# A bidirectional Mamba block with quantized feed-forward: transposes first in TensorE's positions, four evictions behind the next exponential

## What is computed

```python
xz = x @ win.T
u, z = jnp.split(xz, 2, axis=-1)
...
u = jax.nn.silu(jnp.transpose(uc, (0, 2, 1)) + bconv)
dbc = u @ wx.T
...
delta = jax.nn.softplus(dt @ wdt.T + bdt)
A = -jnp.exp(Alog)
dA = jnp.exp(delta[..., None] * A)
dBu = (delta * u)[..., None] * Bm[:, :, None, :]

def step(h, t):
    dA_t, dBu_t, C_t = t
    h = dA_t * h + dBu_t
    return (h, jnp.einsum('bdn,bn->bd', h, C_t))
...
y = jnp.swapaxes(ys, 0, 1) + u * Dp
y = y * jax.nn.silu(z)
return y @ wout.T
```

## Time and profile before

| | us |
|---|---|
| median of 3 runs | 7538.34 |
| lowest, highest | 7523.53, 7542.44 |
| profiled execution | 7536.37 |
| span of the profiled execution | 7534.1 |

### The profile page before, as it was taken

The page is one execution under the profiler, slowest core; times in us unless marked ns, Lnnn a source line. Parts: engine busy times, 40 slices in busy tenths (PEclk is TensorE's granted clock), DMA queues, the critical chain, the costliest instruction groups (busy, mean ns, idle before and its releaser), DMA issues. The chain is left out here.

```text
span 7534.1 us, 111379 instructions
## 1 busy us (share of the span) xinstructions
PE 6807.4 (90%) x32682; PEld 4050.3 (54%) x32682; DVE 6775.4 (90%) x9064; ACT 6168.4 (82%) x13081; POOL 6966.7 (92%) x3774
## 2 busy tenths in 40 slices
PE   6899999999999999999999889999998999998889
PEld 3455555555555555555555555555555555555455
DVE  2799999999999999999999999999999999999766
ACT  1788888888888888888888888888888888888645
POOL 0899999999999999999999999999999999999678
PEclk8999999999999999999999999999999999999999
DMA  8444455444444554444444544444445444444555
GB/s 258 142 138 134 129 147 150 111 139 135 137 134 130 145 151 111 138 138 136 135 131 141 151 116 132 139 137 133 131 141 151 118 131 140 138 133 129 157 187 173
DMA packets 605402, 1064.06 MB, mean 141 GB/s; under 512 B 113584, under 2 KB 221872, under 8 KB 596336
## 3 DMA queue, kind: packets, MB, share of 16 engines
q1 hardware_dynamic: 602704, 1055.81, 48.1%
q10 hardware_dynamic: 2080, 1.05, 0.0%
HBM read 926.59 MB, written 130.03 MB: 140 GB/s over the span
## 5 line engine op out<-in xcount | busy, mean ns | idle before, releaser
L692 POOL TENSOR_TENSOR dBu<-Bb,du 128x1024 f32<-128x1024 f32 x2048 | 4796.6, 2365 | 4.8 <-DMA Bb<-bc_scratch 4.4
L807 ACT ACTIVATE scans<-delta,A 128x512 f32<-128x512 f32 x4096 | 2748.1, 698 | 204.6 <-DVE hC L1162 199.7
L1146 DVE TENSOR_TENSOR_SCAN scans<-scans,state,dBu 128x512 f32<-128x512 f32 x2016 | 2535.4, 1278 | 327.5 <-ACT scans L807 325.0
L1146 DVE TENSOR_TENSOR_SCAN dBu<-scans,state,dBu 128x512 f32<-128x512 f32 x1568 | 1957.0, 1260 | 10.2 <-ACT scans L807 10.2
L1019 PE MATMUL yT<-ident,hC 128*128 128x128 f32 x9216 | 1398.9, 283 | 268.2 <-DVE hC L1162 266.1
L1162 DVE TENSOR_TENSOR hC<-scans,Cb 128x512 f32<-128x512 f32 x2304 | 1553.4, 678 | 4.7 <-PE yT L1019 4.7
L702 POOL TENSOR_TENSOR hR<-dBu,Cb 128x512 f32<-128x512 f32 x1024 | 1307.0, 1276 | 196.0 <-DVE dBu L1146 194.9
L1019 PEld LDWEIGHTS yT<-ident,hC 128*128 128x128 f32 x9216 | 1086.7, 145 | 551.2 <-DVE hC L1162 337.4
L774 ACT ACTIVATE turned<-bg,CT 128x128 f32<-128x128 f32 x3072 | 878.5, 372 | 225.9 <-PE bg L996 225.4
L1012 PE MATMUL bg<-u,comb 128*128 128x512 f32 x2112 | 992.4, 596 | 54.4 <-ACT pre L783 51.6
L973 PE MATMUL bg<-hT,win_z 128*128 128x512 f32 x2048 | 971.7, 597 | 0.0
(11 more groups left out here) (161 smaller groups left out, 7892.4 us busy)
## 6 DMA issues: line engine op xcount, KB each, us to landing
comb<-pre_scratch SPq DMA_DIRECT2D x1040, 256.0 KB, 4.6
Bb<-bc_scratch SPq DMA_DIRECT2D x264, 512.0 KB, 7.1
Cb<-bc_scratch SPq DMA_DIRECT2D x264, 512.0 KB, 7.2
win_u<-in_win SPq DMA_DIRECT2D x264, 256.0 KB, 4.6
pre_scratch<-pre SPq DMA_DIRECT2D x264, 256.0 KB, 3.7
comb<-comb_scratch SPq DMA_DIRECT2D x66, 1024.0 KB, 8.4
win_z<-in_win SPq DMA_DIRECT2D x257, 256.0 KB, 2.7
part_scratch<-pre SPq DMA_DIRECT2D x132, 256.0 KB, 2.0
```

The lines of the kernel that those rows point to most:

```text
L692: pool.tensor_tensor(dBu[:, ring(g, q)], Bb[:, 2 * q:2 * q + 2, :], du[:, j % 2, :].unsqueeze(1).broadcast_to([P, 2, T]), ALU.mult).then_i ...
L807: act.activation(place(n)[:], delta[:, j % 2, :], ACT.Exp, scale=A[:, i % 2, j * N + n:j * N + n + 1]).then_inc(dA_made, 1)
L1146: nc.vector.tensor_tensor_scan(to, place(n)[:], dBu[:, ring(g, q), k, :], state[:, c:c + 1] if i % CH_SEQ else 0.0, ALU.mult, ALU.add).the ...
```

## The change

Two things change, in order alone.

First, `IN_ORDER` puts the entries Y and T of the schedule ahead of all others, and both `background` and the numbering (`BY_END`) go by it. Y was first in its positions already. A T moves ahead of what shared its position in 15 of 24 cases: T1, T17, T33, T49, T65, T81 and T97, which are the first of their tiles and come right after a Y in bank 2, and T5, T9, T25, T37, T57, T101, T105 and T117. T9 is now also taken by ScalarE ahead of O0. Which bank and which earlier user a piece waits for stays as it was (`LAST` still goes by `SCHEDULE`).

Second, `LATER` names the evictions that fall on a table visit, except in the last position: O2 (position 15), U1 (23), C6 (47) and T101 (53). They are now made in the next position, between its two exponentials.

```diff
--- before.py
+++ after.py
@@ -83,7 +83,8 @@
 AT = {name: at for name, at, bank in SCHEDULE}
 BANK = {name: bank for name, at, bank in SCHEDULE}
 
-BY_END = [name for name, at, bank in sorted(SCHEDULE, key=lambda entry: entry[1][-1])]
+IN_ORDER = sorted(SCHEDULE, key=lambda entry: entry[0][0] not in "YT")
+BY_END = [name for name, at, bank in sorted(IN_ORDER, key=lambda entry: entry[1][-1])]
 NUM = {name: e for e, name in enumerate(BY_END)}
 
 LAST = {}
@@ -104,6 +105,7 @@
 GATED = {7: (("Z", 0),), 15: (("Z", 1),), 23: (("Z", 2),), 31: (("C", 0), ("Z", 3)), 39: (("C", 2), ("Z", 4)),
          47: (("C", 4), ("Z", 5)), 53: (("C", 6), ("Z", 6)), 63: (("Z", 7),)}
 assert all(TAKE[f"{kind}{m + (kind == 'C')}"] < p + (kind == "Z") and (kind == "C" or p // NQ == m) for p in GATED for kind, m in GATED[p])
+LATER = [name for name in BY_ACT if TAKE[name] in GATED and TAKE[name] < POS - 1 and name not in URGENT]
 assert sorted(m for p in GATED for kind, m in GATED[p] if kind == "C") == list(range(0, MT, 2))
 assert sorted(m for p in GATED for kind, m in GATED[p] if kind == "Z") == list(range(MT))
 
@@ -891,6 +893,9 @@
                         keep_state(g, j, 2 * q - KEPT_BEHIND)
                         if q == 1:
                             take_yT(g - 1, ready(i - 1, "Y6") if j == 0 else ready(i, f"Y{(j - 2) % MT}"))
+                        for name in LATER:
+                            if p == TAKE[name] + 1:
+                                take(name, i, s, g)
                         if p == TAKE[f"D{m}"] + 1:
                             step_exp(freed(i, f"D{m}"))
                         if p == TAKE[f"D{m}"] + 2:
@@ -911,7 +916,7 @@
                         if p == 12:
                             act.wait_ge(cur_loaded, i * 16 + 32)
                         for name in BY_ACT:
-                            if p == TAKE[name] and name not in URGENT:
+                            if p == TAKE[name] and name not in URGENT and name not in LATER:
                                 take(name, i, s, g)
                         for tt in range(TT):
                             if p == NORM_POS + tt:
@@ -1037,7 +1042,7 @@
 
             def background(i, s, p):
 
-                for name, at, own in SCHEDULE:
+                for name, at, own in IN_ORDER:
                     bank, kind, k = bg[own], name[0], int(name[1:] or 0)
                     for piece in range(len(at)):
                         if at[piece] != p:
```

## The result

The changed kernel takes 7623.3 us (median of 4 runs, 7618.6 to 7631.5), against 7530.9 for the kernel before in the same comparison (7523.1 to 7542.4): the ratio is 1.0124 [1.0107, 1.0141], 92 us slower. The forecast was 7583, so sign and order are right, and the loss is twice the 45 us of the sum. The profiled execution took 7618.6 (span 7616.4).

What follows compares the result with a forecast made beforehand. The period was taken to be set by TensorE's queue, ScalarE's behind it, then VectorE's scans. Earlier transposes, lost cover and moved evictions summed to +1.4 us per chunk, 45 us over 32 chunks: 7583, with 8 in 10 from 7469 to 7680.

Steps and rivals of the forecast that it cites:

- the walk: Tile-by-tile sum through chunk 10 of VectorE's shift against before, positive later, ending at +1.4 us per chunk.
- The term of tile 4: Tile 4: Z4's 1.72 us comes behind T65's gate wait and ahead of U4, taking position 40 from -0.8 to +0.85.
- a rival of its own: TensorE's clock drops after new waits in tiles 1, 4 and 5: 106 us on top, 7689; chance 0.10.
- below 0.96 in the chunks: Sign that the prediction is wrong: the granted clock falls below 0.96 in the chunks.
- The term of tile 0: Tile 0: first transpose finds its gate open, T9 overtakes the last four matmuls of O0; VectorE's shift -0.6 us.
- some 4 to 5: Sign: TensorE's transposes wait some 4 to 5 us per chunk for VectorE's gate, 1.3 or more in tile 1.
- (a): Transposes come 1.72 us earlier; ScalarE's waits of 2.75 and 1.86 us at positions 14 and 30 shrink to under 1.
- (c): Four evictions step behind an exponential; VectorE's waits at positions 16, 24, 48, 54 shrink, O3's wait on TensorE does not.
- costed at 0.1: Tile 6: T105, ahead of a piece of X, waits for T101 to be taken; X is needed only next tile.
- The bound: Upper limit for gate waits at tile heads: 4.7 us per chunk (150 us) if no later slack takes any.
- The faster rival: Idling in tiles 4 and 5 does not reach the scans: -2.15 us per chunk, 7469; chance 0.22.
- the one without change: Only one idling, tile 4's or 5's, reaches the scans; without tile 5's 1.2, +0.2 us per chunk, 7545; chance 0.16.

Runs made afterwards that it cites:

- n = 1 alone: Kernel before, with only the first transpose of each tile moved ahead and the evictions left as they were: 7830.0 us, ratio 1.0403.
- n = 5 and 9 alone: Kernel before, with only the transposes that are not first in their tile moved ahead and the evictions left as they were: 7431.7 us, ratio 0.9866.
- The covered run: Kernel before with only T65 ahead of Z4, plus two matmuls of Z4 made once more ahead of T65: 7573.6 us, ratio 1.0054.
- the best kernel: Kernel before with T5, T9, T25, T37, T57, T101, T117 ahead and U1, C6, T101 evictions moved; T105 behind X: 7388.9 us, ratio 0.9814.

## Why the prediction was right, and where its size was off

VectorE's shift at the places of the walk, forecast and measured (mean over chunks 2 to 29):

| place | forecast | measured | change since the place above: forecast, measured |
|---|---|---|---|
| tile 0, position 8 | -0.6 | +0.14 | -0.6, +0.1 |
| tile 1, position 16 | -0.15 | +0.52 | +0.45, +0.4 |
| tile 2, position 24 | 0 | +0.67 | +0.15, +0.15 |
| tile 3, position 32 | -0.8 | -0.31 | -0.8, -1.0 |
| tile 4, position 40 | +0.85 | +2.21 | +1.65, +2.5 |
| tile 5, position 48 | +1.9 | +2.77 | +1.05, +0.55 |
| tile 6, position 56 | +1.4 | +2.31 | -0.5, -0.45 |
| tile 7, end (the next chunk's first scan) | +1.4 | +2.6 | 0, +0.3 |

**The mechanism.** It held: the heads of the tiles lose their cover, T25 and T57 gain, and the steps of all tiles but 0 and 4 agree within 0.5. The run with n = 1 alone and the one with n = 5 and 9 alone show both parts by themselves, and the gate moved in both orders shows that it is the gate. The wait passes on as forecast: U4's and U6's evictions wait 3.27 and 1.75 us per chunk for TensorE, from 0.83 and 0.62. The size, half of the measured one, holds terms that were too low (tiles 0 and 4) and one that was too high (tile 5), which partly cancel.

**The term of tile 4 was too small.** I priced it as "Z4's 1.72 now comes behind it" at full clock. Measured, tile 4 adds 2.5 per chunk in the changed kernel and 3.05 with T65 alone. From T65 to U4 it takes 3.04 us in the mean in the changed kernel, where the full clock needs 2.21: these 0.83 are the 0.87 that the term was short of. The covered run, where all of it goes, shows that this is the clock. The prediction had that as a rival of its own, with three places at 1.1 us each and 0.10 of the chance. It came true at one of the three: Z1 behind T17's wait of 0.84 and Z5 behind T81's of 0.95 take their 1.88 us in the mean. The Trainium skill's rule on the clock ("TensorE: Matmul & The Clock Gate", section "A second HAM failure mode: psum-queue depth-cycling"), that frequent brief idling between groups of matmuls sends the clock back and forth, fits what tile 4 shows (0.81 over the 9 us of the window above), and O3 in the run with the evictions alone (0.60). In chunk 11 of the changed kernel the one wait of 2.21 us was enough; with T65 alone, waits of 0.89, 0.94 and 1.92 us stand close together. I had set the rule aside because of the mean of 0.98. That was the mistake in method: the clock has to be read behind each new wait, and the mean of the chunk can't show 3 us in 215. The test that I wrote down, "below 0.96 in the chunks", was blind to it too: it stayed at 0.98.

**The term of tile 0 was wrong.** I wrote "its own first T finds the gate open in this chunk" and took it from chunk 10 alone. In the changed kernel T1 waits 0.67 per chunk, 1.41 in the row above; the gain of 0.6 never appeared. It was there to be had: with the same four evictions moved and T9 ahead, but no head ahead, the shift at position 8 is -0.61. What tile 0 lacks passes on, so scan 8 of tile 1 is +2.0 where the walk had +1.15. Tiles 0 and 4 make +1.6 per chunk, tile 7 takes 0.3 more, tiles 5 and 3 give 0.5 and 0.2 back: together 1.2 above the forecast's 1.4, which is the measured 2.6.

**The waits at the gate.** T1, T17, T33, T49, T65, T81 and T97 wait 0.67, 0.84, 0.35, 0.17, 1.92, 0.95 and 0.22 per chunk: 5.1, where "some 4 to 5" was written; tiles 1 and 5 are below their 1.3 and "above 1". (a) was right at T25 (2.75 to 1.03) and at T57 (1.86 to 0.14 per chunk). (c) was right in part. VectorE's waits at positions 16, 24, 48 and 54 shrink, but O3's wait for O2's bank, which was not to shrink, falls from 1.61 to 0.50 per chunk. With all transposes first, or n = 5 and 9 alone, and O2 not moved it is 0: ScalarE waits less for T25 and reaches O2 sooner. So O2's move costs 0.50 there, and at position 16 it has nothing to win: that wait is gone without it too (0.02 per chunk). O3 is stretched by the clock where the evictions move alone (19 chunks), in the changed kernel in none.

**T105 was costed at 0.1.** It waits 2.86 per chunk for ScalarE to take T101 and holds back X. Without that the best kernel gains 21 us (0.7 per chunk). In the changed kernel itself it was not tried.

**The bound was no bound.** 4.7 us per chunk for the heads, "if no later slack takes any of it", was meant as the most. The run with the heads alone reached a shift of 8.7: 0.7, 1.9, 0.9, 0.7, 3.2 and 1.2 in tiles 0 to 5. Tile 4 has the clock (26 of 32 chunks with a stretched Z4), tiles 0 and 3 were left out, and tile 1's head is worth 1.9 where T25 isn't ahead. The faster rival (7469) and the one without change (7545) fell: the idling of tiles 4 and 5 reached the scans, as the rows above show.

## What to carry to other kernels

Moving work ahead in an in-order queue is a gain only if its inputs are there: what it overtook was cover for its wait, and everything behind pays. Split such a rule by what each moved instruction waits for; here the eight moves without a gate ahead win 99 us together, though T105 among them loses, and of the seven others T65 by itself costs more (101 us) than the whole change (92). Price a new idle gap on TensorE not by its length alone, but by the clock of the matmuls behind it, read in windows of a few microseconds; extra matmuls ahead of the wait are a quick test of it.

## What the runs showed of the hardware

- An idle gap costs more than itself. Around and after a wait of 1.92 us in chunk 10 of the run with T65 alone, TensorE ran at 0.62 over 9 us and four matmuls took 3.50 us in place of 1.88; with 1.7 us of unread matmuls in the gap it ran at 1.00, and the kernel was 60 us faster for doing more.
- The same gap does not always do it. T65 waits 2.2 us in most chunks of the changed kernel, and Z4 is stretched in 16 of 32; in the run with T65 alone it is 28 of 32. With a mean wait of 0.85 (gate between the scans) it is none of 32. The wait just ahead goes with it. Where TensorE had also waited 0.81 to 0.94 us at the addition ahead of T65, and T65 then waited 1.83 to 2.23, Z4 is stretched each time (2 chunks of the changed kernel, 21 of the run with T65 alone). Without it, and with a wait of over 2 us at T65, it is 14 of 23 and 7 of 7. What decides among those was not settled.
- The clock already fell in the kernel before, in 6 chunks at Z4 and 5 at O3, and at Z4 not behind one long wait but behind short ones. Where Z4 is stretched, T65 behind it starts 1.0 to 1.1 us after the gate in place of 0.06, and VectorE's scan 8 of the tile comes 0.6 us later than in the other chunks. So the kernel before pays for the clock too. The addition ahead of Z4, Z4 and T65 in chunk 3 of the kernel before:

```profile
981.55 0.63 PE L1019 MATMUL yT<-ident,hC 128*128 128x128 f32 x4 [0.94 <-DVE hC L1162]
982.02 3.56 PE L973 MATMUL bg<-hT,win_z 128*128 128x512 f32 x4
985.37 0.67 PE L996 MATMUL bg<-ident,dBu 128*128 128x128 f32 x4
```
